# Opening of a transformer layer by token halves, on one Trainium2 core

## Chip, core and metric

The kernel runs on one core of one Trainium2 chip. The metric is the device time of one execution in microseconds; less is better. The engines are TensorE (PE, with its weight loads as PEld), VectorE (DVE), ScalarE (ACT), GpSimd (POOL) and SyncE (SP), each with its own instruction stream; data moves through queues of DMAs that the engines issue.

## What is computed

The input `x` has 1024 tokens of 512 features. It is layer-normalised once, and the result feeds two branches whose outputs are added to `x`:

```python
xn = (x - mean(x)) / sqrt(var(x) + 1e-5)
# attention: 32 query heads, 8 key/value heads, head size 16
s = maximum(mean(abs(w), axis=1), 1e-8)          # one magnitude for each output row of w
linear(x, w, scale) = nan_to_num((x @ sign(w / s).T) * (s * scale))
q, k, v = linear(xn, wq, sq), linear(xn, wk, sk), linear(xn, wv, sv)
att = linear(softmax(q @ k.T / 4) @ v, wo, so)
# feed forward, 1792 wide, integer weights -1, 0, 1 with a scale for each row
ffn = (silu(xn @ gate_w.T) * (xn @ up_w.T)) @ down_w.T
out = x + att + ffn
```

## The kernel before

The 1024 tokens are eight row tiles of 128 (TT = 8); a half (HALF) is four tiles, 512 tokens. The normalised input is kept transposed and split in two fp16 parts, `xhi` and `xlo`, and every product with a sign or integer weight is two accumulated matmuls, one on each part. The accumulator memory `ps` has eight banks of 512 fp32 columns.

The order of work of the opening and of the feed-forward part is written out by hand: three strings, `pe_order` (L59), `dve_order` (L62) and `act_order` (L66), list the steps of TensorE, VectorE and ScalarE, and each engine works its list strictly in order. The steps that matter here:

- VectorE: `M` (L731) statistics of one row tile; `H` (L736) and `R` (L742) the inverse standard deviation of four tiles at once, `R` in four dependent small steps; `N` (L752) normalises one tile into `xn`, which has four buffers; `L` (L758) writes `xlo` of a tile. `J` (L773) works out the gain of the feed-forward part in three stages; stage 2 (L784) scales `usc` in three small steps. `S0` (L838) and `Z0` to `Z3` (L846 to L876) work out factors from the magnitudes of the weight rows; `V0` (L909) the factors of the values. `g` and `G` (L885, L891) guard the two halves of a projection against non-finite values, in four instructions each (L796 to L803). `E2` (L830) takes the values out of `ps`. `X` (L894) writes the low fp16 part of a projection, `F` (L900) finishes one unit of the feed-forward part, and `A` (L920) takes a row maximum of the scores (L807).
- ScalarE: `D` (L595) standard deviation of four tiles; `C` (L574, L602) copies a transposed tile out of `ps` to `xhi`; `N` (L607) signs of the weights: N0 for k, N1 for q, N2 for v; `B` (L603) magnitudes of 128 weight rows (Abs with a sum); `F` (L648) the Silu of a feed-forward unit, `E` (L611) a projection out of `ps` to `y`, `X` (L638) its high fp16 part, which is then stored to `q_scratch` or `k_scratch` by SyncE (L411 to L422). `W0` (L623) signs of wo; SyncE loads `wo_rows` and issues the later q stores behind it (L428). The function of the first `F` is in another table than the functions before it.
- TensorE: `X` (L1003) transposes one row tile in four fp32 transposes; `P` (L1052) projects: P0 is k, P1 the first 128 columns of q, P2 v, P3 to P5 the rest of q, 16 matmuls each of 512 columns (v: 64 of 128); `G` and `U` (L1075) are the gate and the up product of one feed-forward unit, eight matmuls each; `F` is both. Unit w is f = w // 2, token half w % 2. `K` (L1011), `S` (L1022) and `Z` (L1034) are tiny products for the factors. `A` (L1104) computes scores for row maxima.
- GpSimd (L503 to L507): waits for the last row tile of `x`, issues the loads of the first gate and up weights, waits for `wq_rows`, and issues three more. Later it writes the low part of each hidden unit (L513).
- SyncE (L391 to L402): issues `x` in eight loads, then wk, wq, wv, the rows of wk, wv and wq, and, once these have landed, wo and the two output scales.

Tile i is transposed into bank i % 4, so X4 waits until L0 has read bank 0. TensorE waits for all eight `xlo` before P0 (L1055), and unit 0 (G0, U0) needs the first four. Units 0 and 1 have banks 4, 5 and 6, 7; the small products have banks 6 (K) and 7 (S, Z).

Of the kernel before, what the change touches and what calls it, by code (L numbers as in the profile page):

```python
# [13 lines left out]
P = 128  # L14
# [13 lines left out]
def layer_kernel(nc, x, wq, wk, wv, wo, wq_rows, wk_rows, wv_rows, wo_rows, sq, sk, sv, so, gate, up, down, sg, su, sd, out,  # L28
                 q_scratch, k_scratch, o_scratch, r_scratch):
    T, H = x.shape  # L30
    HC = H // P
    TT = T // P
# [23 lines left out]

    K_, V_ = "k", "v"
    PROJ = [K_, 0, V_] + list(range(1, QT))
    pe_order = ("K0 K1 X0 X1 X2 X3 X4 X5 X6 X7 G0 P0 P1 S0 Z0 U0 Z1 G1 P2 Z2 P3 U1 F2 F3 F4 P4 P5 F5 F6 A0 F7 A1 A2 "  # L59
                "F8 A3 A4 F9 A5 F10 F11 F12 A6 A7 F13 S1 F14 A8 A9 F15 A10 A11 F16 A12 A13 F17 A14 A15 F18 A16 F19 "  # L60
                "A17 F20 T0 A18 A19 F21 A20 A21 F22 A22 A23 F23 A24 A25 F24 A26 A27 F25 A28 A29 F26 A30 A31 F27 ")
    dve_order = ("M0 M1 J0 M2 J1 M3 H0 M4 R0 M5 N0 N1 M6 M7 L0 H1 N2 R1 N3 N4 L1 N5 L2 N6 N7 L3 L4 L5 L6 L7 J2 S0 Z0 "  # L62
# [3 lines left out]
    act_order = ("D0 C0 C1 D1 N1 C2 N2 C3 N0 C4 B5 C5 C6 C7 B4 B2 B0 B1 B3 F0 E0 E1 F1 X0 X1 F2 E3 F3 V2 X3 F4 E4 E5 "  # L66
                 "F5 F6 X4 F7 F8 F9 W0 F10 X5 F11 Y0 F12 F13 F14 F15 F16 F17 F18 F19 F20 T0 F21 F22 F23 F24 F25 F26 "
                 "F27 ")

# [3 lines left out]
    pe_order, dve_order, act_order = steps_of(pe_order), steps_of(dve_order), steps_of(act_order)  # L73
# [11 lines left out]
    assert [n for kind, n in act_order if kind == "F"] == list(range(FU))  # L85
    VY = PROJ.index(V_) % 2
    WF_BUFS = 4


    NORM = [(t, 0, T) for t in range(QT - 1)] + [(QT - 1, 0, HALF), (QT - 1, HALF, HALF)]  # L90
# [42 lines left out]
    with ExitStack() as ctx:  # L133
# [10 lines left out]
        ps = ctx.enter_context(nc.psum_tensor("ps", [P, 8, 512], F32))  # L144
# [4 lines left out]
        ident = sb("ident", [P, P], F32)  # L149
# [21 lines left out]
        xn = room3[:, 2 * H:6 * H].rearrange("p (b n) -> p b n", b=4)  # L171
# [18 lines left out]
        gain = sb("gain", [P, 4], F32)  # L190
        wf = sb("wf", [P, WF_BUFS, 2, HC * P], F16)
        wd = sb("wd", [P, FT, H], F16)
# [38 lines left out]
        x_loaded = [sem(f"x_loaded{i}") for i in range(TT)]  # L231
# [18 lines left out]
        xhi_ready = sem("xhi_ready")  # L250
        xlo_ready = sem("xlo_ready")
# [25 lines left out]
        usc_ready = sem("usc_ready")  # L277
        proj_ready = sem("proj_ready")
# [8 lines left out]
        vcur_ready = sem("vcur_ready")  # L287
        wf_loaded = [sem(f"wf_loaded{i}") for i in range(WF_BUFS)]
        wd_loaded = sem("wd_loaded")
# [180 lines left out]
        def _(pool):  # L470
# [29 lines left out]
                                    pattern=[[D, HPT]], channel_multiplier=-1).then_inc(pick_ready, 1)  # L500
            nc.gpsimd.memset(vext[:, :, :, :], 1.0).then_inc(consts_ready, 1)

            pool.wait_ge(x_loaded[TT - 1], 16)  # L503
            load_ffn(0)
            pool.wait_ge(rows_q_loaded, 16)
            for f in range(1, WF_BUFS):
# [16 lines left out]
            for w in range(FU):  # L523
                f, hf = w // 2, w % 2
# [41 lines left out]
        def _(act):  # L566
# [7 lines left out]
            def xhi_copy(i):  # L574
                act.wait_ge(xT_ready, i + 1)
                nc.scalar.copy(xhi[:, :, i * P:(i + 1) * P],
                               ps[:, i % 4, :].rearrange("p (c n) -> p c n", c=HC)).then_inc(xhi_ready, 1)

            weights = [(wk_loaded, NH * D, KV), (wq_loaded, 0, NH * D), (wv_loaded, NH * D + KV, KV)]

# [136 lines left out]
        def _(dve):  # L717
# [40 lines left out]
            def x_low(i):  # L758
                dve.wait_ge(xhi_ready, i + 1)
                nc.vector.tensor_tensor(xlo[:, :, i * P:(i + 1) * P],  # L760
                                        ps[:, i % 4, :].rearrange("p (c n) -> p c n", c=HC),
                                        xhi[:, :, i * P:(i + 1) * P], ALU.subtract).then_inc(xlo_ready, 1)

            steps = 0
# [46 lines left out]
            for kind, n in dve_order:  # L811
# [88 lines left out]
                elif kind == "F":  # L900
                    f, hf = n // 2, n % 2
# [99 lines left out]
        def _(pe):  # L1001
            pe.wait_ge(consts_ready, 1)
            def transpose_x(i):  # L1003
                pe.wait_ge(xn_ready, i + 1)
                if i >= 4:
                    pe.wait_ge(xlo_ready, i - 3)
                for c in range(HC):
                    mm = nc.tensor.transpose(ps[:, i % 4, c * P:(c + 1) * P], xn[:, i % 4, c * P:(c + 1) * P], ident[:, :])
                mm.then_inc(xT_ready, 1)

            def spread_gain(stage):  # L1011

                if stage == 0:
                    pe.wait_ge(gain_ready, 1)
                    nc.tensor.transpose(ps[0:1, 6, 0:P], gain[:, 0:1], ident[:, :]).then_inc(gainT_ready, 1)
                else:
                    pe.wait_ge(gmax_ready, 1)
                    pe.wait_ge(consts_ready, 2)
                    nc.tensor.matmul(ps[:, 6, P:P + 1], ones[0:1, :], gain[0:1, 1:2], start=True,
                                     stop=True).then_inc(gspread_ready, 1)  # L1020
# [28 lines left out]
                                     head_diag[:, :, :].rearrange("q t h -> q (t h)"), start=True,  # L1049
                                     stop=True).then_inc(spread_ready, 1)  # L1050

            def project(n):  # L1052
                what = PROJ[n]
                pe.wait_ge(sign_ready, SIGNS.index({K_: 0, V_: 2}.get(what, 1)) + 1)
                pe.wait_ge(xlo_ready, TT)  # L1055
                if n >= 2:
                    pe.wait_ge(y_ready, n - 1)
                if what == V_:
                    for k in range(TT):
                        for c in range(HC):  # L1060
                            for xs in (xhi, xlo):
                                mm = nc.tensor.matmul(bank_pair(n % 2)[:, k * KV:(k + 1) * KV], xs[:, c, k * P:(k + 1) * P],  # L1062
                                                      sgn[:, c, NH * D + KV:NQKV], start=(c == 0 and xs is xhi),
                                                      stop=(c == HC - 1 and xs is xlo))
                else:
                    c0 = NH * D if what == K_ else what * P
                    for hf in range(2):
                        for c in range(HC):
                            for xs in (xhi, xlo):
                                mm = nc.tensor.matmul(ps[:, 2 * (n % 2) + hf, :], sgn[:, c, c0:c0 + P],  # L1070
                                                      xs[:, c, hf * HALF:(hf + 1) * HALF],
                                                      start=(c == 0 and xs is xhi), stop=(c == HC - 1 and xs is xlo))
                mm.then_inc(proj_ready, 1)

            def feed_forward(w, z):  # L1075
                f, hf = w // 2, w % 2
                if z == 0:
                    pe.wait_ge(wf_loaded[f % WF_BUFS], 32 * (f // WF_BUFS + 1))
                    pe.wait_ge(xlo_ready, HALF // P if w == 0 else TT)
                    if w == 1:  # L1080
                        pe.wait_ge(usc_ready, 1)
                    if w >= 2:
                        pe.wait_ge(h_ready, w - 1)
                    if w == T_AT + 1:
                        pe.wait_ge(max_taken, 1)
                elif w == 1:
                    pe.wait_ge(factors_ready, 2)
                    pe.wait_ge(out_factors_ready, 2)
                for c in range(HC):
                    for xs in (xhi, xlo):  # L1090
                        mm = nc.tensor.matmul(ps[:, 4 + 2 * (w % 2) + z, :], wf[:, f % WF_BUFS, z, c * P:(c + 1) * P],  # L1091
                                              xs[:, c, hf * HALF:(hf + 1) * HALF],
                                              start=(c == 0 and xs is xhi), stop=(c == HC - 1 and xs is xlo))
                mm.then_inc((gate_ready, up_ready)[z], 1)
# [18 lines left out]
            for kind, n in pe_order:  # L1113
                if kind == "X":
                    transpose_x(n)
                elif kind == "K":
                    spread_gain(n)
                elif kind == "P":
                    project(n)
                elif kind == "S":  # L1120
                    sum_magnitudes(n)
                elif kind == "Z":
                    head_factors(n)
                elif kind in "GU":
                    feed_forward(n, "GU".index(kind))
                elif kind == "F":
                    feed_forward(n, 0)
                    feed_forward(n, 1)
                elif kind == "A":
                    if n == 0:  # L1130
                        pe.wait_ge(y_ready, len(PROJ))
                        pe.wait_ge(kA_loaded[0], 32)
                    if n % UNITS == 0:
                        pe.wait_ge(q_loaded[0][n // UNITS], 32)
                    if n == SUM_AT:
                        pe.wait_ge(factors_ready, 3)
                    rows(n, 0, n // UNITS, n % UNITS)
                elif kind == "T":
                    pe.wait_ge(h_ready, T_AT)
                    transpose_max(0, 0, 6)  # L1140
# [171 lines left out]
```

## Time and profile before

| | |
|---|---|
| median of 3 runs | 516.37 us (515.12 to 516.67) |
| span of the profiled execution, first to last instruction | 512.5 us |
| PE busy | 484.8 us, 95% |
| DVE busy | 417.1 us, 81% |
| ACT busy | 352.3 us, 69% |
| POOL busy | 92.9 us, 18% |
| DMA read and written | 33.24 MB and 10.35 MB |

The profile gives the span of the profiled execution and not its device time; the median of the runs is 3.9 us above that span. The span cut in 40 equal slices of 12.8 us, with the busy share in tenths and the granted clock of TensorE (PEclk), looks so (first seven slices, read from the page): PE 1 8 9 9 9 9 9 (the eighth 5), ACT 1 9 3 3 5 3 3, DVE 7 7 7 9 7 6 7, DMA 8 9 4 4 7 4 6. Only the eighth slice has a granted clock below full.

### The profile page before, as it was taken

How to read it: one execution, taken by the hardware profiler on the slowest of the kernel's cores; microseconds unless marked ns; L12 is line 12 of the kernel's file. 1: busy time of each engine (PE TensorE's matmuls, PEld its weight loads, DVE VectorE, ACT ScalarE, POOL GpSimd, SP SyncE). 2: the span in 40 equal slices, each digit the busy share in tenths (PEclk: the TensorE clock that was granted, in tenths of full speed). 3: DMA queues.
4: the chain of work that ended last, by engine and by line, in shares of the span. 5: the costliest groups of instructions: out<-in, count | busy, mean ns of one | idle time of the engine just before them, and what ended most of it. 6: DMA issues, size and time to landing. Idle time of an engine off the chain costs nothing.

```text
span 512.5 us, 9735 instructions
## 1 busy us (share of the span) xinstructions
PE 484.8 (95%) x3882; PEld 160.6 (31%) x3882; DVE 417.1 (81%) x487; ACT 352.3 (69%) x655; POOL 92.9 (18%) x138
## 2 busy tenths in 40 slices
PE   1899999599999999999999999999999999999996
PEld 1464444234332222222222222222222222223442
DVE  7779767566778999999999999999999962223985
ACT  1933533522337999999999999999999997774000
POOL 4213242333424000000000000000000103241021
PEclk9999999799999999999999999999999999999999
DMA  8944746422100911202102111120120114452321
GB/s 272 276 74 116 157 68 167 132 51 42 23 0 5 166 39 41 61 24 57 44 24 62 40 32 53 41 59 25 42 59 24 53 29 121 98 155 83 106 71 54
DMA packets 31300, 38.99 MB, mean 76 GB/s; under 512 B 6608, under 2 KB 20816, under 8 KB 31256
## 3 DMA queue, kind: packets, MB, share of 16 engines
q1 hardware_dynamic: 22232, 27.34, 18.7%
q0 software_dynamic: 8304, 10.95, 11.5%
q8 instruction: 31, 0.51, 0.4%
q10 hardware_dynamic: 720, 0.08, 0.1%
q14 instruction: 13, 0.11, 0.1%
HBM read 33.24 MB, written 10.35 MB: 85 GB/s over the span
## 4 chain that ended last, share of the span: by engine, by line
PE 82%; ACT 9%; DVE 3%; DMA 3%; issue 2%; SPq 0%; ACTq 0%; DVEq 0%
PE ps L1219 25%; PE ps L1091 17%; PE ps L1184 15%; PE ps L1152 10%; PE ps L1100 9%; ACT room L674 6%; PE ps L1070 3%; PE ps L1245 3%; DMA q_scratch<-parts 2%; ACT osb L685 1%; DMA hlo<-x 1%; DVE stats L733 1%; DVE room L755 1%; PE ps L1062 1%; PE ps L1111 1%
## 5 line engine op out<-in xcount | busy, mean ns | idle before, releaser
L807 DVE TENSOR_REDUCE nmx<-ps 128x1 f32<-128x1024 f32 x256 | 293.5, 1215 | 12.8 <-PE ps L1100 12.5
L674 ACT ACTIVATE room<-ps 128x512 f32<-128x512 f32 x512 | 274.3, 596 | 21.3 <-PE ps L1184 11.2
L1219 PE MATMUL ps<-room,vcur 128*32 128x256 f32 (+1 forms) x1912 | 160.0, 406 | 4.4 <-ACT osb L685 4.2
L1100 PE MATMUL ps<-kA,qst 48*128 48x512 f16 x512 | 145.6, 383 | 5.6 <-DVE nmx L807 5.6
L1184 PE MATMUL ps<-qst,kB 50*128 50x512 f16 x512 | 149.5, 383 | 0.8 <-DVE room L906 0.5
L1091 PE MATMUL ps<-room,wf 128*128 128x512 f16 x448 | 102.4, 384 | 0.0
L1219 PEld LDWEIGHTS ps<-room,vcur 128*32 128x32 f32 x1912 | 37.6, 107 | 99.7 <-issue 52.6
L1184 PEld LDWEIGHTS ps<-qst,kB 50*128 50x128 f16 x512 | 30.8, 93 | 112.5 <-ACT room L674 100.9
L1091 PEld LDWEIGHTS ps<-room,wf 128*128 128x128 f16 x448 | 42.7, 99 | 56.3 <-issue 9.6
L655 ACT ACTIVATE room<-ps,gsc 128x512 f32<-128x512 f32 x28 | 19.2, 686 | 58.4 <-PE ps L1091 58.4
L513 POOL TENSOR_TENSOR hlo<-room,hhi 128x512 f16<-128x512 f32 x28 | 33.4, 1193 | 95.5 <-ACT hhi L585 95.5
L519 POOL TENSOR_TENSOR shp<-mxs,ones 16x128 f16<-16x128 f32 x16 | 7.2, 452 | 226.9 <-ACT mxs L591 226.9
L1152 PE MATMUL ps<-wd,hhi 128*128 128x512 f16 x112 | 42.5, 380 | 0.0
L1152 PE MATMUL ps<-wd,hlo 128*128 128x512 f16 x112 | 42.5, 380 | 0.0
L906 DVE SCALAR_TENSOR_TENSOR room<-ps,usc,room 128x512 f32<-128x512 f32 x28 | 20.9, 746 | 21.2 <-issue 9.3
L1100 PEld LDWEIGHTS ps<-kA,qst 48*128 48x128 f16 x512 | 27.2, 94 | 13.4 <-issue 7.5
L942 DVE TENSOR_TENSOR y<-y,ga 128x1024 f32<-128x1024 f32 (+1 forms) x5 | 5.1, 1010 | 29.3 <-DMA ga<-r_scratch 29.3
L1070 PE MATMUL ps<-room,sgn 128*128 128x512 f16 x80 | 17.8, 379 | 0.0
L644 ACT ACTIVATE parts<-y,q_up 128x1024 f16<-128x1024 f32 x4 | 4.6, 1148 | 19.1 <-DMA q_scratch<-parts 9.7
L585 ACT CAST hhi<-room 128x512 f16<-128x512 f32 x28 | 17.1, 611 | 0.6 <-DVE room L906 0.6
L479 POOL TENSOR_TENSOR room<-room,parts 128x512 f32<-128x512 f32 x7 | 9.6, 1367 | 39.6 <-DVE room L954 27.9
L1152 PEld LDWEIGHTS ps<-wd,hhi 128*128 128x128 f16 x112 | 10.9, 98 | 13.2 <-issue 1.8
(127 smaller groups left out, 271.8 us busy)
## 6 DMA issues: line engine op xcount, KB each, us to landing
qst<-q_scratch SPq DMA_DIRECT2D x32, 192.0 KB, 3.6
o_scratch<-osb SPq DMA_DIRECT2D x16, 256.0 KB, 2.3
q_scratch<-parts SPq DMA_DIRECT2D x12, 256.0 KB
hlo<-x SPq DMA_DIRECT2D x8, 256.0 KB, 4.5
parts<-x POOLq DMA_DIRECT2D x8, 256.0 KB, 3.8
wf<-gate POOLq DMA_DIRECT2D x14, 128.0 KB, 3.8
wf<-up POOLq DMA_DIRECT2D x14, 128.0 KB, 4.9
wd<-down POOLq DMA_DIRECT2D x1, 1792.0 KB, 13.7
```

Of the source, the lines that this page charges most:

```text
L513: nc.gpsimd.tensor_tensor(hlo[:, f, hf * HALF:(hf + 1) * HALF], hb[:, w % 2, :], hhi[:, f, hf * HALF:(hf + 1) * HALF], ALU.subtract).then_ ...
L585: nc.scalar.copy(hhi[:, f, hf * HALF:(hf + 1) * HALF], hb[:, n % 2, :]).then_inc(hhi_ready, 1)
L655: nc.scalar.activation(gt[:, n % 2, :], ps[:, 4 + 2 * (n % 2), :], ACT.Silu, scale=gsc[:, f:f + 1]).then_inc(gt_ready, 1)
L674: nc.scalar.activation(probs[:, s % 2, r, :], ps[:, score_bank(entry(j, i)), :], ACT.Exp, scale=gam_reg[par][r]).then_inc(scores_free, 1)
L807: nc.vector.tensor_reduce(nmx[:, hf, idx:idx + 1], bank_pair(idx % 2), AX.X, ALU.max, negate=True).then_inc(rows_free, 1)
L906: nc.vector.scalar_tensor_tensor(out=hb[:, n % 2, :], in0=ps[:, 5 + 2 * (n % 2), :], scalar=usc[:, f:f + 1], in1=gt[:, n % 2, :], op0=ALU. ...
L1070: mm = nc.tensor.matmul(ps[:, 2 * (n % 2) + hf, :], sgn[:, c, c0:c0 + P], xs[:, c, hf * HALF:(hf + 1) * HALF], start=(c == 0 and xs is xhi ...
L1091: mm = nc.tensor.matmul(ps[:, 4 + 2 * (w % 2) + z, :], wf[:, f % WF_BUFS, z, c * P:(c + 1) * P], xs[:, c, hf * HALF:(hf + 1) * HALF], star ...
L1100: return nc.tensor.matmul(ps[:, 2 * (idx % 2) + b, :], qst[low:low + KROWS, par, hf, head, qt * P:(qt + 1) * P], kA[low:low + KROWS, par, ...
L1152: mm = nc.tensor.matmul(ps[:, i, :], (hhi, hlo)[part][:, f, i * P:(i + 1) * P], wd[:, f, :], start=(f == 0 and part == 0), stop=(f == FT - ...
L1184: nc.tensor.matmul(ps[:, score_bank(e), :], kB[low:low + SROWS, par, kt % (TT // 2) * P:(kt % (TT // 2) + 1) * P], qst[low:low + SROWS, pa ...
L1219: mm = nc.tensor.matmul(ps[32 * r:32 * r + 32, 7, of], vcur[:, par, key_tile(r, j), :], probs[:, s % 2, r, of], start=(j == 0 and part == ...
```

## The change

The second group of row tiles is moved behind three groups of matmuls on the first four. On TensorE X0 to X3 are followed by G0, U0 and a new step p0 (the first token half of P0), then X4 to X7, p1 (the first half of P1), and then P0 and P1 with their second halves alone. U0 had stood behind Z0; G1 now stands ahead of Z1. On VectorE J2, M4 and M5 change places with R0 and N0 to N3, L0 to L3 come together, and M6, M7, H1 and R1 follow them. On ScalarE C0 to C3 stand together, then the three signs, B5 and D1, then C4 to C7, then the other five B. Tiles 4 to 7 are transposed into banks 1, 6, 3, 7. G1 no longer waits for `usc`; X5 does. GpSimd waits for row tile 5, not 7, before the first feed-forward loads.

```diff
-    pe_order = ("K0 K1 X0 X1 X2 X3 X4 X5 X6 X7 G0 P0 P1 S0 Z0 U0 Z1 G1 P2 Z2 P3 U1 F2 F3 F4 P4 P5 F5 F6 A0 F7 A1 A2 "
+    pe_order = ("K0 K1 X0 X1 X2 X3 G0 U0 p0 X4 X5 X6 X7 p1 P0 P1 S0 Z0 G1 Z1 P2 Z2 P3 U1 F2 F3 F4 P4 P5 F5 F6 A0 F7 A1 A2 "
...
-    dve_order = ("M0 M1 J0 M2 J1 M3 H0 M4 R0 M5 N0 N1 M6 M7 L0 H1 N2 R1 N3 N4 L1 N5 L2 N6 N7 L3 L4 L5 L6 L7 J2 S0 Z0 "
+    dve_order = ("M0 M1 J0 M2 J1 M3 H0 J2 R0 N0 N1 N2 N3 M4 L0 L1 L2 L3 M5 M6 M7 H1 R1 N4 N5 L4 N6 N7 L5 L6 L7 S0 Z0 "
                  "g0 V0 Z1 G0 F0 Z2 g1 X0 Z3 G1 E2 F1 X1 g2 F2 G2 F3 g3 G3 X3 F4 g4 F5 G4 A0 F6 F7 A1 A2 A3 F8 A4 F9 "
...
-    act_order = ("D0 C0 C1 D1 N1 C2 N2 C3 N0 C4 B5 C5 C6 C7 B4 B2 B0 B1 B3 F0 E0 E1 F1 X0 X1 F2 E3 F3 V2 X3 F4 E4 E5 "
+    act_order = ("D0 C0 C1 C2 C3 N0 N1 N2 B5 D1 C4 C5 C6 C7 B4 B2 B0 B1 B3 F0 E0 E1 F1 X0 X1 F2 E3 F3 V2 X3 F4 E4 E5 "
...
+    X_BANK = [0, 1, 2, 3, 1, 6, 3, 7]
...
-            pool.wait_ge(x_loaded[TT - 1], 16)
+            pool.wait_ge(x_loaded[TT - 3], 16)
...
-                               ps[:, i % 4, :].rearrange("p (c n) -> p c n", c=HC)).then_inc(xhi_ready, 1)
+                               ps[:, X_BANK[i], :].rearrange("p (c n) -> p c n", c=HC)).then_inc(xhi_ready, 1)
...
-                                        ps[:, i % 4, :].rearrange("p (c n) -> p c n", c=HC),
+                                        ps[:, X_BANK[i], :].rearrange("p (c n) -> p c n", c=HC),
...
                 if i >= 4:
-                    pe.wait_ge(xlo_ready, i - 3)
+                    pe.wait_ge(xlo_ready, 4)
+                if X_BANK[i] == 6:
+                    pe.wait_ge(usc_ready, 1)
                 for c in range(HC):
-                    mm = nc.tensor.transpose(ps[:, i % 4, c * P:(c + 1) * P], xn[:, i % 4, c * P:(c + 1) * P], ident[:, :])
+                    mm = nc.tensor.transpose(ps[:, X_BANK[i], c * P:(c + 1) * P], xn[:, i % 4, c * P:(c + 1) * P], ident[:, :])
...
-            def project(n):
+            def project(n, halves=(0, 1)):
...
-                pe.wait_ge(xlo_ready, TT)
+                pe.wait_ge(xlo_ready, TT if 1 in halves else TT // 2)
...
-                    for hf in range(2):
+                    for hf in halves:
...
-                mm.then_inc(proj_ready, 1)
+                if 1 in halves:
+                    mm.then_inc(proj_ready, 1)
...
-                    if w == 1:
-                        pe.wait_ge(usc_ready, 1)
...
+                elif kind == "p":
+                    project(n, (0,))
                 elif kind == "P":
-                    project(n)
+                    project(n, (1,) if ("p", n) in pe_order else (0, 1))
```

## Rows read from the trace of the kernel before

**Rows 1.** Windows: start:end, length, busy us (instructions) by engine, PEclk, DMA share, GB/s.
```profile
15.00:20.00 5.00, 4.24 (x24) 3.40 (x23) 4.93 (x12) 4.88 (x10) 0.03 (x1) 1.00 0.89 279
20.00:25.00 5.00, 4.96 (x25) 2.12 (x24) 3.20 (x13) 4.94 (x13) 3.15 (x6) 1.00 0.82 249
```

**Rows 2.** Timeline: normalising, transposes and copies of the opening (start us, us, engine, line).
```profile
9.13 0.14 DVE L746 RECIPROCAL rstd<-std 128x4 f32<-128x4 f32 x1
...
10.73 0.97 DVE L755 TENSOR_SCALAR room<-hlo,mv,rstd 128x512 f32<-128x512 f32 x2
...
11.30 1.97 PE L1008 MATMUL ps<-ident,room 128*128 128x128 f32 x8 [3.42 <-DVE room L755]
...
12.45 0.59 ACT L576 CAST room<-ps 128x512 f16<-128x512 f32 x1 [4.06 <-PE ps L1008]
...
19.57 0.63 PE L1008 MATMUL ps<-ident,room 128*128 128x128 f32 x4 [0.49 <-DVE room L760]
```

**Rows 3.** Lines in 8 to 35 us: busy us, mean ns of one, idle before.
```profile
L760 DVE TENSOR_TENSOR room<-ps,room 128x512 f16<-128x512 f32 x8 | 5.1, 678 | 0.0
...
L610 ACT ACTIVATE sgn<-room 128x512 f16<-128x512 f32 (+1 forms) x3 | 3.2, 1056 | 0.0
```

**Rows 4.** Timeline: ScalarE and VectorE from the last two Abs to V0.
```profile
22.57 0.62 ACT L606 ACTIVATE qst<-qst 128x512 f32<-128x512 f32 x1
...
23.18 0.62 ACT L606 ACTIVATE qst<-qst 128x512 f32<-128x512 f32 x1
...
25.79 1.11 ACT L621 ACTIVATE y<-ps,cqk 128x1024 f32<-128x1024 f32 x1
26.93 0.43 DVE L796 TENSOR_SCALAR gr<-y 128x512 f32<-128x512 f32 x1 [1.90 <-ACT y L621]
...
28.32 0.73 DVE L803 COPY_PREDICATED y<-gb,ga 128x512 f32<-128x512 uint8 x1
...
30.15 0.29 DVE L914 TENSOR_TENSOR svb<-ps,svb 128x128 f32<-128x128 f32 x1 [1.09 <-PE ps L1040]
```

**Rows 5.** Timeline: TensorE and VectorE after V0.
```profile
31.65 0.08 PEld L1045 LDWEIGHTS ps<-ident,both 128*4 128x4 f32 x1 [0.35 <-DVE both L856]
...
33.48 3.74 PE L1062 MATMUL ps<-sgn,room 128*128 128x128 f16 x64
...
39.51 0.16 DVE L874 SCALAR_TENSOR_TENSOR q_up<-ps,q_div 128x4 f32<-128x4 f32 x1
...
40.95 12.25 PE L1091 MATMUL ps<-room,wf 128*128 128x512 f16 x56
...
47.90 0.74 DVE L906 SCALAR_TENSOR_TENSOR room<-ps,usc,room 128x512 f32<-128x512 f32 x1
```

**Rows 6.** Timeline and queries by line L392, L483: loads of x and wf.
```profile
10.10 0.70 POOL L482 DMA_DIRECT2D wf<-gate  x1 [4.74 <-DMA hlo<-x]
...
L392 SPq DMA_DIRECT2D hlo<-x x8: 380/432/432, 1.2 to 4.4; - x8
DMA to landing us min/median/max: 2.6/4.5/5.4
...
DMA to landing us min/median/max: 7.0/7.0/7.0
```

**Rows 7.** Query by line L1008, two stretches: duration ns min/median/max, starts.
```profile
L1008 PE MATMUL ps<-ident,room x4: 421/421/474, 14.6 to 15.3; 128*128 128x128 f32 x4
...
L1008 PE MATMUL ps<-ident,room x5: 272/273/332, 18.0 to 18.8; 128*128 128x128 f32 x5
```

**Rows 8.** Chain of waits around the later stall: start us, us, what.
```profile
78.59 1.82 ACT sgno L625
...
82.11 9.91 DMA q_scratch<-parts
```

**Rows 9.** Timeline: TensorE after that stall.
```profile
95.83 0.61 PE L1100 MATMUL ps<-kA,qst 48*128 48x512 f16 x2 [5.62 <-DVE nmx L807]
...
96.36 5.25 PE L1091 MATMUL ps<-room,wf 128*128 128x512 f16 x16
```

## The prediction

> **What bounds the kernel now.** I read the windows first: over 15 to 25 us TensorE (PE) is nearly full, and so is ScalarE (ACT), 9.82 of 10 us [rows 1]. So the opening has two full engines, not one. The timeline says why: ACT has the xhi copies (C), the sign passes (N) and the magnitudes (B, Abs) in one row. TensorE starts transposing at 11.30 and pays 1.97 us for two tiles, later 0.63 for one [rows 2]. From 40.95 it runs without a gap [rows 5] up to a wait near 90 us, in which the chain names the stores of q_scratch [rows 8] and TensorE sits idle for 5.62 us [rows 9]. Behind TensorE's order stands a chain of factors: last Abs, table load and F0, E0 (ends 26.90), guard g0 on VectorE (DVE) at 26.93, V0, then Z1, whose result TensorE takes at 31.65 [rows 4, 5]. That PE row has 0.35 us idle put down to Z1: the chain is already level with TensorE. Work that TensorE does early is worth only what this chain allows.
>
> All sums are made against one profiled execution, of which the profile gives the span, 512.5 us. The median of the runs, 516.37, is 3.9 above it, and I carry that as it is. About 0.3% (1.5 us) is what a measurement of this kernel tells from no change.
>
> **The change, step by step.**
>
> First half, DVE. M4 and M5 leave the way of R0 and N0; J2 enters. One M (M5) and the four steps of R0 lie between 9.13 and N0 at 10.73 [rows 2]: 0.8 for an M and 0.2 for a small step. J2 is three such steps, 0.6. Without M4, R0 could start at 9.13 - 0.8 = 8.33, with J2 at 8.95; four steps later N0 starts at 9.75 instead of 10.73: 1.0 us sooner, and X0 at 10.3. Two tiles took 1.97 us [rows 2], so X0 to X3 end near 14.1, with C3 (0.59) at 14.7 and L3 (0.68 [rows 3]) at 15.3. The other X_BANK numbers cost nothing: banks 6 and 7 are empty here, and J2, for which X5 waits, is long done.
>
> G0's data. POOL issued the first wf loads at 10.10, when x tile 7 had landed. Tile 5 is the sixth of eight issues from 1.2 to 4.4, so issued at 3.5, and takes about 4.9 (between median 4.5 and maximum 5.4): it lands at 8.4, and the load goes out 1.45 sooner. "up" took 7.0 us to land under full DMA, from 10.80 to 17.8 [rows 6]; with the same duration it lands at 16.35. Bounds: below, the fastest landing of x, 2.6, which makes L3 (15.3) the limit; above, no gain, 17.8, since the engines are saturated. I take 16.35, by the nearest row. So G0 waits a microsecond beyond L3.
>
> TensorE then has G0, U0, p0, 24 matmuls at 0.219 (12.25/56 [rows 5]): 5.25 us. The same transposes took 421 ns at 14.6 to 15.3 us and 272 at 18.0 to 18.8 [rows 7]: TensorE was slow for its first microseconds of work. If it becomes quick at the same moment, near 17.3, G0's first matmuls run at about 0.43; I take 0.6 us for that, between 0 and 1.9 (the longest slow stretch is that behind the stall, where most of 16 matmuls in 5.25 us ran at half speed [rows 9]). X4 starts at 16.35 + 5.25 + 0.6 = 22.2. Before, X7 began at 19.57 [rows 2].
>
> Is the second half ready by then? On ACT the three signs (3.2 us by their mean [rows 3]) and B5 now stand ahead of D1, from 14.7 on, so D1 is at about 18.4 and R1 done at 19.5: N4 and N5 are ready. But DVE's order is N4 N5 L4 N6 N7, so N6 sits behind L4: X4 0.65, C4 0.6, L4 0.7, N6 0.5, N7 0.5, X7 0.65, C7 0.6, in all 4.2 us: C7 ends at 26.4. ACT is idle from D1 to C4, some 4 us, while it had been full [rows 1]; that idle time is what the change costs.
>
> Then five Abs (B4 B2 B0 B1 B3) follow C7 at 0.61 each [rows 4], the last starting at 26.4 + 4 x 0.61 = 28.9; before, at 23.18. From there rows 4 and 5 give fixed distances: last Abs to g0 3.75 (table load, F0, E0), g0 to its end 2.12, V0 to Z1 on TensorE 1.50, then 0.15 to P2. P2 starts at 28.9 + 7.5 = 36.4 where it started at 33.48. Before, V0 had waited for TensorE until 30.15 [rows 4]; that cushion of 1.1 us is used up, so DVE shifts by more, from 30.15 to 34.8, 4.6 us.
>
> TensorE itself: X7 ends near 25.8, p1, P0 and P1 (24 matmuls) 31.1, S0 and Z0 to 32.2, G1 34.0. It then waits 2.3 us for Z1. Behind Z1 are queued P2, Z2, P3, U1, everything.
>
> Further on DVE is dense up to 56 us. U1 needs Z3, which ended at 39.67 (39.51 + 0.16), so 44.3, against U1's start at 40.95: shift 3.4. F4 needs DVE's F2, 48.64 + 4.6 = 53.25; TensorE arrives at 44.35 + 40 x 0.219 = 53.1 [rows 5]: another 0.15. Behind that both have slack and the shift stays with TensorE: **3.6 us**.
>
> The later stall does not swallow it: the stores start when the sign of wo (78.59 [rows 8]) has been taken, which stands behind F9's work on ACT and so moves with TensorE.
>
> Nothing is removed: the same instructions are issued in another order. Forecast 516.4 + 3.6 = 520.0.
>
> **Rivals.**
>
> 1. The new gap of 2.3 us, or the wait for wf before G0, costs speed as well. For it: behind the 5.62 us gap 16 matmuls took 5.25 us instead of 3.5 [rows 9]. Against it: this gap is less than half as long. Price: up to those 1.8 us, so 521.8. Chance 0.20. [...]
>
> 2. The wf load lands before 15.3 and TensorE is quick by then. X4 starts at 20.6, all behind it 1.6 us sooner: 518.4. For it: several queues share the engines, and a load issued sooner may get its share sooner. Against: DMA share 0.89 over 15 to 20 us, and 7.0 us to land. Chance 0.12.
>
> 3. Faster: in case 2 G1 ends at 34.0 - 1.6 = 32.4, or 1.1 before P2's old start at 33.48. If Z1 is ready by then, TensorE's lead comes through whole: 515.3. The point that decides is the last Abs: Z1 reaches TensorE 7.4 us behind it, so it must start by 25.0. In the diff five Abs stand behind C7, and C7 behind X7, which is later than before. Chance 0.06.
>
> 4. No change: the delay arises as computed but ends in a wait. TensorE has 5.62 us of idle near 90 us; if the stores that end it are set by the queues and not by the sign of wo, it shrinks by the delay: 516.4. For it: the chain has 9.91 us of DMA there [rows 8]. Against: they start only when the sign is done. Chance 0.10.
>
> **How the numbers follow.** The forecast has 0.52; its own range is 518.3 to 521.6. The range reaches down from the forecast past case 2 and up past case 1: 517.4 to 522.6, which leaves out cases 3 and 4 and some of the tails. Faster by over 0.3%: 0.06 (case 3). Within: 0.10 (case 4). Slower: 0.84.
>
> **What would show it.** Right: N0 near 9.75 and X0 near 10.3; G0 waiting for DMA until about 16.4; ACT with an idle stretch of 3 to 4 us before C4; last Abs near 29; g0 near 32.6; TensorE idle about 2.3 us with Z1 (L856) as releaser; P2 at 36.4 and U1 at 44.3 released by DVE; the later stall again 5.6 us long, 3.6 later. Wrong: last Abs before 25, or a Z1 that TensorE does not wait for; a stall near 90 us that is shorter than before by the delay.

## The result, and the profile after

| | before | changed |
|---|---|---|
| median | 515.75 us (4 runs, 513.96 to 516.67) | 519.86 us (4 runs, 519.18 to 520.34) |
| span of the profiled execution | 512.5 us | 518.4 us |
| PE, DVE, ACT busy | 484.8, 417.1, 352.3 us | 488.0, 417.6, 352.4 us |

The ratio is 1.0088, with a 95% interval of 1.0056 to 1.0121: slower by about 4 us. The profiled execution after took 520.09 us, 1.7 above its span. Every other run of the kernel before that has both numbers shows the same 1.7 to 1.8 (514.22 us with a span of 512.5, for one), so the profiled execution of before took about 514.2 us and was among the shorter ones; the two spans therefore lie further apart (5.9 us) than the medians (4.1).

First the timeline of the changed kernel, in the order in which the prediction went through it:

```profile
9.42 0.56 POOL L484 DMA_DIRECT2D wf<-up  x1
9.56 2.02 DVE L756 TENSOR_SCALAR room<-hlo,mv,rstd 128x512 f32<-128x512 f32 x4
...
10.28 3.52 PE L1011 MATMUL ps<-ident,room 128*128 128x128 f32 x16 [2.60 <-DVE room L756]
...
16.23 5.31 PE L1093 MATMUL ps<-room,wf 128*128 128x512 f16 x16 [2.43 <-DMA wf<-up]
...
23.74 1.07 ACT L577 CAST room<-ps 128x512 f16<-128x512 f32 x2 [5.57 <-PE ps L1011]
...
25.56 1.11 PE L1011 MATMUL ps<-ident,room 128*128 128x128 f32 x8 [1.42 <-DVE room L756]
...
29.68 0.62 ACT L607 ACTIVATE qst<-qst 128x512 f32<-128x512 f32 x1
...
33.42 0.43 DVE L797 TENSOR_SCALAR gr<-y 128x512 f32<-128x512 f32 x1 [1.95 <-ACT y L622]
...
36.93 0.27 PE L1048 MATMUL ps<-ident,both 128*4 128x128 f32 x1 [2.25 <-DVE both L857]
```

N0 starts at 9.56 and X0 at 10.28, a microsecond sooner than in [rows 2]. Then TensorE waits 2.43 us for the load of "up", which was issued at 9.42. G0 and U0, 16 matmuls, take 5.31 us. ScalarE sits idle 5.57 us ahead of C4, TensorE 1.42 us ahead of X6. The last Abs starts at 29.68 (23.18 in [rows 4]), g0 at 33.42 (26.93), and Z1 comes to TensorE at 36.93 (31.65 in [rows 5]), after an idle time of 2.25 us where 0.35 had stood.

The windows show how full the engines are now; the columns are those of [rows 1]:

```profile
15.00:20.00 5.00, 3.77 (x11) 1.48 (x12) 4.20 (x14) 3.17 (x5) 0.00 (x0) 0.69 0.83 314
20.00:25.00 5.00, 4.14 (x23) 2.16 (x20) 0.72 (x3) 1.07 (x2) 3.17 (x6) 0.97 0.80 234
```

ScalarE is busy 3.17 and 1.07 us in the two stretches in which it had been busy 4.88 and 4.94. The work it has not done by then stands behind C7.

TensorE behind Z1, in its own timeline:

```profile
37.04 5.36 PE L1065 MATMUL ps<-sgn,room 128*128 128x128 f16 x64
...
46.13 12.25 PE L1093 MATMUL ps<-room,wf 128*128 128x512 f16 x56
...
100.66 0.61 PE L1102 MATMUL ps<-kA,qst 48*128 48x512 f16 x2 [5.28 <-DVE nmx L808]
101.20 5.82 PE L1093 MATMUL ps<-room,wf 128*128 128x512 f16 x16
```

P2 (37.04) takes 5.36 us where it had taken 3.74, and U1 starts at 46.13 instead of 40.95. Z3's last step and F2 in VectorE's timeline:

```profile
44.79 0.16 DVE L875 SCALAR_TENSOR_TENSOR q_up<-ps,q_div 128x4 f32<-128x4 f32 x1
...
53.09 0.73 DVE L907 SCALAR_TENSOR_TENSOR room<-ps,usc,room 128x512 f32<-128x512 f32 x1
```

Z3 came at 44.79 (39.51 before), a lag of 5.3, and F2 at 53.09 (47.90), a lag of 5.2. TensorE's lag of 5.18 us at U1 stays nearly whole through the stall near 100 us: the row maximum there is released after 5.28 us of idle time, 5.62 in [rows 9], and starts 4.83 us later than before. The 16 matmuls behind it take 5.82 instead of 5.25.

The granted clock of TensorE in those stretches (start:end, length, busy us, PEclk, DMA share, GB/s):

```profile
16.00:18.00 2.00, 1.77 (x6) 0.73 1.05 409
18.00:20.00 2.00, 2.00 (x6) 0.50 0.47 179
...
37.00:38.00 1.00, 1.00 (x14) 0.70 0.07 16
38.00:39.00 1.00, 1.00 (x12) 0.50 0.00 0
```

The granted clock reads 0.50 from about 16.9 us (1.00 until then gives the 0.73 of the first row) to about 20, and again from 37.4 on. Slow and quick, below, are read from durations: of the 16 matmuls of G0 and U0 a slow matmul took up to 634 ns and a quick one 379; a transpose took 421 or 272 ns, a matmul of P2 314 or 219. These are the lengths of single records, which overlap; quick matmuls of 512 columns follow each other every 0.219 us. Each time in this execution the reading fell less than a microsecond after TensorE had gone back to work behind an idle stretch: G0 starts at 16.23 and P2 at 37.04.

### The profile page after: what moved, and what is told of

It is laid out like the page before. It is cut to its first block, busy times and chain, and to the rows that moved or that the text cites. A ratio compares the mean times of both kernels' runs of the same rounds, so it can differ in the third digit from the quotient of the medians.

```text
span 518.4 us, 9739 instructions
## 1 busy us (share of the span) xinstructions
PE 488.0 (94%) x3882; PEld 162.6 (31%) x3882; DVE 417.6 (81%) x487; ACT 352.4 (68%) x655; POOL 92.7 (18%) x138
## 4 chain that ended last, share of the span: by engine, by line
PE 68%; ACT 18%; DMA 8%; issue 3%; DVE 2%; SPq 1%; ACTq 0%; POOL 0%; DVEq 0%
PE ps L1223 19%; PE ps L1093 17%; ACT room L675 15%; PE ps L1188 11%; PE ps L1156 7%; PE ps L1102 7%; PE ps L1249 3%; PE ps L1073 2%; DMA q_scratch<-parts 2%; DMA o_scratch<-osb 2%; ACT osb L686 1%; DMA wf<-up 1%; PE ps L1065 1%; DMA hlo<-x 1%; DMA ga<-r_scratch 1%
## 5 line engine op out<-in xcount | busy, mean ns | idle before, releaser
L675 ACT ACTIVATE room<-ps 128x512 f32<-128x512 f32 x512 | 274.2, 597 | 21.2 <-PE ps L1188 11.2
L1093 PE MATMUL ps<-room,wf 128*128 128x512 f16 x448 | 104.5, 390 | 2.4 <-DMA wf<-up 2.4
L480 POOL TENSOR_TENSOR room<-room,parts 128x512 f32<-128x512 f32 x7 | 9.6, 1367 | 39.5 <-DVE room L955 27.3
```

What stands on the lines that cost most here:

```text
L675: nc.scalar.activation(probs[:, s % 2, r, :], ps[:, score_bank(entry(j, i)), :], ACT.Exp, scale=gam_reg[par][r]).then_inc(scores_free, 1)
```

## The experiments

Each kernel was run beside the kernel before on the same chip, 6 to 12 times. Runs of one kernel differ by some us. The granted clock goes with it in part: of the 33 runs of the kernel before that stood beside e9 to e12, the three shortest (513.7 to 513.9) have a mean granted clock of 0.997, the five longest (518.9 to 519.4) one of 0.984. It is not shown to be the whole of it: ten of the twelve runs of e1 read 0.993, and they lie between 514.4 and 519.3. So ratios to the kernel before are the measure here, and the timelines tell where time went. A ratio differs from the quotient of the two medians by up to 0.25% (e12), and a difference below about 1.5 us is not resolved. The changed kernel stands at 1.0088 in the first comparison, and at 1.0076 in e9.

**e1: four of the five Abs into ScalarE's idle stretch.**

```diff
-... N0 N1 N2 B5 D1 C4 C5 C6 C7 B4 B2 B0 B1 B3 F0
+... N0 N1 N2 B5 D1 B0 B1 B2 B3 C4 C5 C6 C7 B4 F0
```

> Edit of the changed kernel (519.9): four of the five Abs behind C7 are put into ScalarE's idle stretch between D1 and C4. Theory 1 (the loss comes down ScalarE: late C7, then five Abs, then F0, E0, g0, V0, Z1): the last Abs starts 2.4 us sooner, Z1 reaches TensorE as G1 ends, the gap of 2.25 us is gone: 517.6. Theory 2 (that gap also costs the clock in P2, 5.36 us for 3.74): P2 is quick as well, another 1.6 us off: 516.0. Rival (the loss lies in the first microseconds of TensorE, the wait for wf and the slow G0, U0): no change, 519.9.

Measured: 516.82 us, ratio 1.0026 (1.0002 to 1.0050). ScalarE's timeline, then TensorE's:

```profile
24.50 1.07 ACT L577 CAST room<-ps 128x512 f16<-128x512 f32 x2 [2.34 <-PE ps L1011]
...
27.98 0.64 ACT L607 ACTIVATE qst<-qst 128x512 f32<-128x512 f32 x1
```

```profile
35.66 0.27 PE L1048 MATMUL ps<-ident,both 128*4 128x128 f32 x1 [0.22 <-DVE both L857]
35.77 3.74 PE L1065 MATMUL ps<-sgn,room 128*128 128x128 f16 x64
...
43.83 4.48 PE L1093 MATMUL ps<-room,wf 128*128 128x512 f16 x20 [0.43 <-DVE q_up L875]
```

The Abs now stand ahead of C4; one is left, at 27.98. X0 started 0.9 us later in this execution (11.19), G0 starts at 16.76, and even so Z1 is there at 35.66, after 0.22 us of idle time. The gap is gone and P2 takes 3.74 us. By the ratios about 6 of the 8.8 parts in 1000 are back, some 3 us; by the medians (516.82 against 514.83 before, where the changed kernel lay 4.1 above) it is 2 us. So one line of order on ScalarE carries between a half and two thirds of the loss. A new wait shows: U1 waits 0.43 us for Z3's q_up.

**e2: N6 and N7 ahead of L4.**

```diff
-... R1 N4 N5 L4 N6 N7 L5 L6 L7 S0
+... R1 N4 N5 N6 N7 L4 L5 L6 L7 S0
```

> Edit of the changed kernel (519.9): N6 and N7 stand ahead of L4 on VectorE. Theory 1: TensorE's 1.4 us wait ahead of X6 goes, C7, the last Abs, g0, Z1 and P2 all come about 1.3 us sooner, the gap before Z1 stays as long as it was: 518.6. Rival (the wait before X6 is covered, as P0 waits for L7 anyway or Z1 is set elsewhere): 519.9.

Measured: 518.95 us, ratio 1.0080 (1.0047 to 1.0114), over 8 runs from 516.45 to 523.32.

```profile
22.96 1.91 PE L1011 MATMUL ps<-ident,room 128*128 128x128 f32 x16
...
35.24 0.27 PE L1048 MATMUL ps<-ident,both 128*4 128x128 f32 x1 [2.03 <-DVE both L857]
```

X4 to X7 are one piece of 1.91 us; the 1.42 us ahead of X6 are gone, and Z1 comes at 35.24, 1.7 us sooner than in the profile after, with a gap of 2.03 us still there. In the timeline the theory holds; the median does not resolve the 1.3 us.

**e3: both.**

> Both edits. Theory 1 with 2: 1.3 and 3.9 us add up, 514.7, level with the kernel before or just under it; theory 1 without the clock: 516.3. Rival (the two are one and the same slack, only the longer counts): 516.0, as with the Abs alone.

Measured: 516.15 us, ratio 1.0020 (1.0004 to 1.0036).

```profile
32.94 0.27 PE L1048 MATMUL ps<-ident,both 128*4 128x128 f32 x1 [0.21 <-DVE both L857]
33.05 3.73 PE L1065 MATMUL ps<-sgn,room 128*128 128x128 f16 x64
...
41.11 7.07 PE L1093 MATMUL ps<-room,wf 128*128 128x512 f16 x32 [0.43 <-DVE q_up L875]
```

Z1 comes at 32.94, P2 starts at 33.05, 0.4 us sooner than in the kernel before (33.48). None of it is left at U1: 41.11 against 40.95, because U1 waits for Z3 on VectorE. In the profiles the two edits add up: G0 to Z1 is 20.70 us in the profile after, 1.80 less in e1, 1.55 less in e2 (which has G0 at 16.09) and 3.45 less here (G0 at 15.69). The time does not show that sum: 516.15 is not the expected 514.7 but what the rival and the theory without the clock had given (516.0 and 516.3), and the ratio (1.0020 after 1.0026) is only a small step beyond e1.

**e4: the wf loads wait for the last row tile again.**

```diff
-pool.wait_ge(x_loaded[TT - 3], 16)
+pool.wait_ge(x_loaded[TT - 1], 16)
```

> Edit of the changed kernel (519.9): GpSimd waits for the last row tile again before the first loads of wf, as in the kernel before. Theory 1 (G0 waits for wf, and all behind it): up lands at 17.8 and not 16.2, G0 and all behind it 1.5 us later: 521.4. Theory 2 (the clock rises at a moment set by how long TensorE has worked, so G0 and U0 are slow all the same): 521.4 as well; if it rises at a fixed moment near 20 us instead, fewer matmuls are slow and it costs only 0.7: 520.6. Rival (the wait is covered by the second half, which is late anyway): 519.9.

Measured: 523.16 us, ratio 1.0169 (1.0137 to 1.0201): not 1.5 but 3.3 us (medians) to 4.2 us (ratios) more than the changed kernel.

```profile
18.26 6.40 PE L1093 MATMUL ps<-room,wf 128*128 128x512 f16 x16 [3.52 <-DMA wf<-up]
```

G0 starts at 18.26, 2.0 us later: "up" was issued at 11.2 instead of 9.4 and took 7.0 us to land. The 16 matmuls take 6.40 us, 1.1 more than in the profile after; the two together are the 3.1 us by which the spans differ (521.5 and 518.4). In this execution the wait cost its length and a longer slow stretch behind it: the matmuls still took 634 ns each beyond 22.4 us, which speaks against a fixed moment near 20 us at which TensorE becomes quick. P2 is slow here too, 5.36 us behind an idle time of 2.25.

**e5: fill the wait ahead of G0.** Eight transposes of the identity into bank 7, between X3 and G0.

> Edit of the changed kernel (519.9; kernel before 514.8 in the last comparison): eight transposes of the identity into the empty bank 7 fill TensorE's wait for wf ahead of G0; their output is not used. They take 1.8 us of a wait of 2.4, so by themselves they cost nothing. Clock theory: TensorE has worked without a gap since X0, G0 and U0 take 3.5 us and not 5.3, all behind them comes 1.8 us sooner: 518.1. Rival (the clock rises at its own moment, whatever TensorE did in between): 519.9.

Measured: 519.45 us, ratio 1.0063 (1.0037 to 1.0088), 4 of the 11 runs at 516.7 to 517.2 and 6 at 519.2 to 519.7.

```profile
14.17 1.04 PE L1122 MATMUL ps<-ident 128*128 128x128 f32 x8
...
15.87 3.63 PE L1093 MATMUL ps<-room,wf 128*128 128x512 f16 x16 [0.67 <-DMA wf<-up]
```

The eight transposes took 1.04 us, not the 1.8 expected: TensorE was quick at 14.17 already, at 272 ns for each. 0.67 us of wait are left, and G0 and U0 take 3.63 us and not 5.31. That the fill did it is not shown, for G0 and U0 are as quick without a fill in e6, e8 and e10. The time moved by less than the 1.8 us expected, and its interval reaches that of the changed kernel. Ahead of Z1 this execution has the same idle time of 2.25 us, and P2 takes 3.74.

**e6: fill the gap ahead of Z1.** Nine matmuls into bank 0 behind a wait for E0.

```diff
-... S0 Z0 G1 Z1 P2
+... S0 Z0 G1 Y0 Z1 P2
...
+elif kind == "Y":
+    pe.wait_ge(y_ready, 1)
+    for c in range(9):
+        nc.tensor.matmul(ps[:, 0, :], sgn[:, 0, 0:P], xhi[:, 0, 0:HALF], start=True, stop=True)
```

> Edit of the changed kernel (519.9): nine matmuls of 512 columns into the free bank 0 ahead of Z1, in the gap that TensorE has there; their output is not used. They take 1.95 us and can start once E0 has read the bank, 1.2 us before G1 ends. Clock theory: P2 takes 3.7 us and not 5.4, but U1 waits for Z3 anyway (VectorE is dense there), so at most about 1.2 of the 1.6 us comes through: 518.7. Rival (P2's slowness is hidden whole behind VectorE's chain to Z3): 519.9.

Measured: 519.19 us, ratio 1.0087 (1.0058 to 1.0116).

```profile
16.16 3.61 PE L1093 MATMUL ps<-room,wf 128*128 128x512 f16 x16 [1.49 <-DVE room L761]
...
35.28 0.27 PE L1048 MATMUL ps<-ident,both 128*4 128x128 f32 x1 [0.31 <-DVE both L857]
35.39 3.74 PE L1065 MATMUL ps<-sgn,room 128*128 128x128 f16 x64
```

The idle time ahead of Z1 is down to 0.31 us and P2 takes 3.74. The median lies between the two numbers expected and the ratio is that of the changed kernel, so the test does not decide. In this execution G0 and U0 were quick without any help, and U1 starts at 43.46, 2.7 us sooner than in the profile after, yet the span of 517.2 us is only 1.2 shorter: the 16 matmuls behind the later stall took 6.04 us, and the granted clock read less than full once more between 160 and 170 us (0.83 on average). What the opening gains, later stretches can take back.

**e7: wf loads behind row tile 3.**

```diff
-pool.wait_ge(x_loaded[TT - 3], 16)
+pool.wait_ge(x_loaded[3], 16)
```

> Edit of the changed kernel (519.9): GpSimd waits for row tile 3, not 5, before the first loads of wf, which go out about 1.5 us sooner. Theory 1: up lands at 14.8, G0 starts at 15.3 when L3 is done, 1 us sooner, and a shorter gap keeps the clock: with G0 and U0 still slow 518.9, quick 517.1. Rival (the DMA engines are full; wf then lands hardly sooner and the rows of wq, wv later, which delays B5 and D1): 519.9 to 520.5.

Measured: 518.70 us, ratio 1.0052 (1.0028 to 1.0076).

```profile
15.47 5.53 PE L1093 MATMUL ps<-room,wf 128*128 128x512 f16 x16 [1.49 <-DMA wf<-up]
...
36.53 5.33 PE L1065 MATMUL ps<-sgn,room 128*128 128x128 f16 x64
```

G0 at 15.47 instead of 16.23, G0 and U0 slow, P2 slow: the case "518.9" of the expectation. "up" was issued at 8.1 us and took 7.3 to land, so it landed 0.8 us sooner.

**e8: e3 and e7 together.**

> The Abs in ScalarE's idle stretch, N6 and N7 ahead of L4, and the early wf loads together (the first two gave 516.2 against 514.8 before). Theory 1: another 1 us off, 515.1. Rival (with the Abs moved, TensorE is no longer waited for by anything that matters, because g0, V0 and Z3 set U1): unchanged, 516.2.

Measured: 514.97 us, ratio 0.9998 (0.9975 to 1.0021): level with the kernel before. TensorE first, then ScalarE:

```profile
15.17 3.61 PE L1093 MATMUL ps<-room,wf 128*128 128x512 f16 x16 [1.49 <-DMA wf<-up]
...
25.00 3.61 PE L1073 MATMUL ps<-room,sgn 128*128 128x512 f16 x16 [1.02 <-DVE room L761]
...
31.58 0.27 PE L1048 MATMUL ps<-ident,both 128*4 128x128 f32 x1 [0.21 <-DVE both L857]
...
39.75 8.58 PE L1093 MATMUL ps<-room,wf 128*128 128x512 f16 x39 [0.43 <-DVE q_up L875]
```

```profile
19.92 0.63 ACT L607 ACTIVATE qst<-qst 128x512 f32<-128x512 f32 x1 [0.95 <-DMA qst<-wq_rows]
...
23.67 0.66 ACT L607 ACTIVATE qst<-qst 128x512 f32<-128x512 f32 x1
```

P2 begins 1.8 us before that of the kernel before. Now ScalarE waits 0.95 us for the rows of wq, which land at 19.9, TensorE waits 1.02 us for L7, and U1 0.43 us for Z3; the lead at U1 is 1.2 us.

**e9: the changed kernel once more.**

> The changed kernel itself once more, beside the others on the same chip, because the runs of one kernel fall into clusters some 2 us apart and four runs are few: about 519 to 520 against 515 before; among its profiles some should show G0 and U0 or P2 quick, and be shorter by 1.6 to 1.8 us for each, if the clock makes the clusters.

Measured: 519.46 us (10 runs, 516.86 to 523.58), ratio 1.0076 (1.0043 to 1.0110).

```profile
16.26 5.18 PE L1093 MATMUL ps<-room,wf 128*128 128x512 f16 x16 [2.44 <-DMA wf<-up]
...
36.83 0.27 PE L1048 MATMUL ps<-ident,both 128*4 128x128 f32 x1 [2.25 <-DVE both L857]
36.93 3.74 PE L1065 MATMUL ps<-sgn,room 128*128 128x128 f16 x64
...
44.99 3.18 PE L1093 MATMUL ps<-room,wf 128*128 128x512 f16 x14 [0.43 <-DVE q_up L875]
```

The same gap of 2.25 us, and P2 quick: U1 starts 8.06 us behind P2, where it had been 9.09 in the profile after, because it waits for Z3. A slow P2 costs 1.0 us of its 1.6, and the span is 1.4 us shorter (517.0 for 518.4). The ten runs spread from 516.9 to 523.6 without clear clusters; that the clock makes the spread stays unproven.

**e10: e8 with Z3 ahead of X0 on VectorE.**

```diff
-... Z2 g1 X0 Z3 G1 E2
+... Z2 g1 Z3 X0 G1 E2
```

> The kernel with the Abs in the idle stretch, N6 and N7 ahead of L4 and the early wf loads (515.0), and Z3 ahead of X0 on VectorE. Theory: U1 waited 0.43 us for Z3, which stood behind X0's 1.27 us: 514.5. Rival: F4 then waits for F2 on VectorE instead, since X0 is only put behind: 515.0.

Measured: 515.67 us, ratio 1.0016 (0.9984 to 1.0049), beside a kernel before at 515.91.

```profile
39.16 8.80 PE L1093 MATMUL ps<-room,wf 128*128 128x512 f16 x40
...
48.48 3.61 PE L1093 MATMUL ps<-room,wf 128*128 128x512 f16 x16 [0.52 <-DVE room L907]
...
94.28 0.61 PE L1102 MATMUL ps<-kA,qst 48*128 48x512 f16 x2 [5.19 <-DVE nmx L808]
```

U1's wait for Z3 is gone (39.16 against 39.75). The rival's wait has come in its place: F4 waits 0.52 us for F2 on VectorE and starts at 48.48, against 48.69 after a wait of 0.15 in e8, so 0.2 of the 0.6 us is left. The later stall ends 0.4 us sooner than in e8 (94.67 there). The matmuls behind it take 5.79 us, 5.35 in e8, which gives it back; the two profiled spans are equal, 511.5. Not resolved by the medians.

**e11: e10 with idle work for TensorE.** Transposes of the identity into bank 7: 18 at the start, 8 behind K1, 6 ahead of G0.

> The same with idle work for TensorE: 18 transposes of the identity into bank 7 at the start, 8 behind K1, 6 ahead of G0; none of them is used. Clock theory: X0 to X3 take 2 us and not 3.5, G0 and U0 are quick in every run, and the slow cluster of runs goes: 513.3. Rival (the chain over the last Abs, which waits for the rows of wq at 19.9, sets U1 whatever TensorE does): 514.5, only with less spread.

Measured: 514.19 us, ratio 0.9976 (0.9945 to 1.0008), lowest run 512.11; beside it the kernel before 515.91. The best of all, though the interval still holds 1.

```profile
1.59 4.10 PE L1122 MATMUL ps<-ident 128*128 128x128 f32 x18 [1.59 <-POOL ident L488]
...
7.87 1.97 PE L1122 MATMUL ps<-ident 128*128 128x128 f32 x8
10.43 3.67 PE L1011 MATMUL ps<-ident,room 128*128 128x128 f32 x16 [0.58 <-DVE room L756]
```

The 18 and 8 transposes were slow, at medians of 418 and 421 ns, and X0 to X3 still take 3.67 us, at a median of 421: the warming did not do what was expected of it. G0 and U0 were quick (3.61 us), as they are in e10 without it. The slow runs did not go either: the twelve reach from 512.1 to 518.3.

**e12: the kernel before with the first two groups of idle work.**

> The kernel before with the same idle work ahead of X0 (18 and 8 transposes into bank 7, not used). If TensorE's slow first microseconds bound the old opening, X0 to X3 are quicker and it gains up to 1.5 us: 513.5. If ScalarE binds it, which is full from 12.4 to 23.9 us, it gains at most the 0.5 us by which C0 comes sooner: 514.7 against 515.0.

Measured: 515.17 us against 515.91, ratio 1.0011 (0.9982 to 1.0040): no change, as ScalarE's bound says, but the test is weak, for X0 and X1 were not made quicker:

```profile
7.99 1.11 PE L1120 MATMUL ps<-ident 128*128 128x128 f32 x8
11.76 1.97 PE L1008 MATMUL ps<-ident,room 128*128 128x128 f32 x8 [2.66 <-DVE room L755]
```

The eight transposes took 1.11 us here, at a median of 273 ns, and the granted clock reads 0.97 over 8 to 9 us; then TensorE was idle 2.66 us, and X0 and X1 took 1.97 us as before, 421 ns for a transpose, with a granted clock of 0.50 ahead of them:

```profile
9.00:11.00 2.00, 0.10 (x1) 0.50 1.10 363
```

## Why the prediction was right, point by point

- **N0, X0, wf.** Forecast 9.75, 10.3, 16.35; in the profile 9.56, 10.28, and G0 at 16.23. The landing estimate, the old duration from the new issue, held within 0.15 us: "up" took 6.8 us to land, 7.0 in [rows 6].
- **G0 and U0.** Taken as 0.6 us over the quick rate, bounds 0 to 1.9; it was 1.8 (5.31 against 3.5). This is the term of the sum that was sized wrong, close to its upper bound, and its reason was another: the forecast had TensorE slow without a break until about 17.3. But eight transposes at 14.17 in e5 took 272 ns each, and in the profile after the granted clock fell to 0.50 at about 16.9, behind the wait for wf. The upper bound, 1.9, leaned on the stall of [rows 9], behind which only about half of the 16 matmuls were slow: seven took 609 to 634 ns, and the other nine, from 99.3 us on, a median of 379. Over the profiles it varies: 3.6 us in e6, e8, e10 and, with fills, in e5 and e11; 5.2 to 5.5 in the profile after and in e1, e2, e3, e7 and e9; 6.4 in e4.
- **N6 behind L4.** Forecast C7 4.2 us behind X4; X4 started at 23.11, C7 ended near 27.3: 4.2. e2 shows the cause.
- **ScalarE's idle stretch.** Forecast some 4 us, 5.57 in the profile: X4 came 0.9 us later than forecast, and D1 ended sooner, at 18.17. e1 is the test: with Abs in it, the gap before Z1 is gone, and between a half and two thirds of the loss.
- **Last Abs to P2.** Forecast 7.5 us; 29.68 to 37.04 is 7.4, with a table load of 1.28 us in it, as in the kernel before. Gap before Z1: 2.3 forecast, 2.25 found.
- **U1 and F4.** Forecast a shift of 3.4 at U1, set by VectorE. e9 shows that wait, 0.43 us for q_up. In the profile after it is hidden, as P2 was slow, and the shift is 5.18. Of the 1.8 us beyond the forecast, 0.8 is there at the last Abs already (29.7 for 28.9, from the slow G0 and U0) and 1.0 is the slow P2's.
- **The later stall** absorbed next to nothing: 5.28 against 5.62 us, and 4.8 us later. Rival 4 is out.
- **Rival 1** (the new gaps cost speed) occurs, together with the forecast's chain and not instead of it, in some executions. It was priced at 1.8 us in one place; it has two places, worth 0.8 and 1.0 us beyond the forecast at U1, both of them in the profile after, where the granted clock reads 0.50 at 18 to 20 and at 38 to 39 us. What takes the speed away and what brings it back is not shown by any run. That stops of about 2.3 us can be enough was an estimate from the one gap of 5.62 us in [rows 9], and it holds only at times: in e9, behind the same gap of 2.25 us, the granted clock reads 1.00 over 36 to 40 us and P2 takes 3.74 us.
- **Rival 3** (a lead that comes through) is what e3 and e8 build by hand: P2 at 33.05 and 31.69. Its deciding point, a last Abs by 25.0, is met in e8 (23.67), and P2 is 1.8 us early there.
- **The total.** Forecast 3.6 us on 516.37; measured 4.1 us and, in e9, 3.6 (519.46 against 515.91). The two profiled executions lie further apart, 5.9 us. That 520.0 and 519.86 agree so closely is in part luck: the slow matmuls were priced low, at 0.6 us for 1.8 at G0 and U0 and at nothing for P2, while the median on which the sum was put was 0.6 us above the one measured beside the changed kernel.

What stays open: what makes up the last microsecond or so between e3 (1.0020) and e8 (0.9998), where wf came sooner and G0 and U0 happened to be quick in the profile, and whether it is there at all, for the intervals overlap; how much of the spread of the runs is the clock's; why the same gap costs speed in one execution and not in another; and whether e11 beats the kernel before.

## What to carry to other kernels

When one engine's late work is pulled forward, look at the engine that feeds the next stage: here TensorE had work for its idle time, but ScalarE was full as well, and holding its copies back behind TensorE's new work left it idle for 5.57 us with five magnitudes still to do. Move the independent work of that engine into the hole in the same edit; here that, with N6 ahead of L4 and earlier loads, brought the new order level with the old one (e8, 0.9998) and not below it. With strict orders, a single step that waits (L4 ahead of N6) holds up steps that need nothing from it, and a gap on TensorE can have a price beyond its length: behind 2.25 us ahead of Z1, P2 took 5.36 us in the profile after and 3.74 in e9.

## What the runs showed of the hardware

- Behind an idle gap of the same length, TensorE is quick in one execution and slow in another: after 2.25 us ahead of Z1, P2 took 5.36 us in the profile after and in e4 and 5.33 in e7, and 3.74 in e5 and e9; after about 1.5 us ahead of G0, G0 and U0 took 5.53 (e7) and 3.61 (e6).
- The longest gap ahead of G0 had the longest slow stretch behind it, 3.52 us and 6.40 us for the 16 matmuls (e4). Among the shorter gaps there is no such order: 5.31 us behind 2.43 in the profile after, 5.54 behind 1.90 in e1, 5.53 behind 1.49 in e7.
- In e11 TensorE stayed slow through 18 transposes in 4.10 us, 8 in 1.97 and 16 in 3.67 (medians of 418, 421 and 421 ns), with gaps of 0.6 to 0.7 us between them; six at 13.89 us took 0.86, at a median of 273 ns. In e12 the same first 18 were followed by 8 in 1.11 us, and after 2.66 us of idle time the next 8 took 1.97 again.
- The granted clock reads 1.00 in e9 over 16 to 20 us, while its 16 matmuls took 5.18 us. The first stretch has 1.74 us of work in 5 matmuls; at 0.219 us each, 8 would fit. The profile after reads 0.73 and 0.50 over the same two stretches, although it has 6 matmuls in the first:

```profile
16.00:18.00 2.00, 1.74 (x5) 1.00 1.05 407
18.00:20.00 2.00, 2.00 (x8) 1.00 0.58 220
```

Over these stretches that column and the durations do not agree, and slow and quick are said here by the durations: in e9 the five matmuls that start in the first stretch took 609 to 634 ns each, under a reading of 1.00.
